# Two weight splits moved behind four bank sums, and the last norm's variance computed with tokens on partitions

## The reference

```python
attn = softmax((x @ Wq) @ (x @ Wk).T * scale) @ (x @ Wv) @ Wp + bp
cms  = gelu(attn @ cW1 + cb1) @ cW2 + cb2 + one_hot(codes)      # hidden size 2048
mod  = gelu(concat(attn, cms) @ mW1 + mb1) @ mW2 + mb2
x    = clip(x + cms + mod, 0, 1)

h    = x + gelu(x @ Wd[role] + bd) @ Wu[role] + bu              # adapter, 256 wide
mean = h.mean(-1); var = ((h - mean) ** 2).mean(-1)
x    = (h - mean) * rsqrt(var + 1e-5) * gamma[role] + beta[role]
```

## Time and profile before

| | |
|---|---|
| median of three runs | 2097.38 us (2095.5 to 2100.05) |
| the profiled execution | 2097.53 us |
| its span, first to last instruction | 2095.8 us |
| mean granted TensorE clock | 0.998 |
| TensorE matmul busy | 2073.3 us (99%), 9128 records |
| VectorE busy | 1588.5 us (76%) |
| ScalarE busy | 1097.1 us (52%) |
| GpSimd busy | 701.6 us (33%) |

### The profile page before, as it was taken

The page is one execution under the profiler, slowest core; times in us unless marked ns, Lnnn a source line. Parts: engine busy times, 40 slices in busy tenths (PEclk is TensorE's granted clock), DMA queues, the critical chain, the costliest instruction groups (busy, mean ns, idle before and its releaser), DMA issues.

```text
span 2095.8 us, 25018 instructions
## 1 busy us (share of the span) xinstructions
PE 2073.3 (99%) x9128; PEld 1701.9 (81%) x9128; DVE 1588.5 (76%) x1929; ACT 1097.1 (52%) x1625; POOL 701.6 (33%) x690
## 2 busy tenths in 40 slices
PE   9999999999999999999999999999999999999997
PEld 7887888888888888888888888888888888888884
DVE  4358878777868878867787887977686888787776
ACT  5366645454447654544454755544444666454444
POOL 1254415674002331766100332455400042165510
PEclk9999999999999999999999999999999999999999
DMA  8895444543212425444403222322130423421111
GB/s 304 239 236 143 133 114 120 130 119 101 103 46 105 154 76 138 114 113 103 129 30 133 88 71 83 99 61 61 45 127 0 151 74 104 115 61 59 52 61 41
DMA packets 183993, 221.94 MB, mean 106 GB/s; under 512 B 10288, under 2 KB 148272, under 8 KB 179776
## 3 DMA queue, kind: packets, MB, share of 16 engines
q1 hardware_dynamic: 175776, 184.58, 27.1%
q0 software_dynamic: 6720, 29.47, 7.8%
q10 hardware_dynamic: 1376, 6.29, 0.8%
HBM read 199.33 MB, written 62.91 MB: 125 GB/s over the span
## 4 chain that ended last, share of the span: by engine, by line
PE 93%; DVE 4%; ACT 1%; DMA 1%; issue 1%; SPq 0%; ACTq 0%; DVEq 0%
PE bank L864 30%; PE bank L866 30%; PE bank L865 30%; PE bank L919 1%; DMA stage<-ready_up 1%; DVE ring L1757 1%; DVE pc L2032 1%; PE bank L1262 1%; DVE xs L2207 0%; ACT ring L1298 0%; DMA fold_staging<-fold_w 0%; DVE ph_lo L2015 0%; PE bank L1233 0%; PE bank L1232 0%; PE bank L1231 0%
## 5 line engine op out<-in xcount | busy, mean ns | idle before, releaser
L1757 DVE TENSOR_TENSOR ring<-stage,ring 128x1024 fp32r<-128x1024 f32 (+1 forms) x288 | 356.1, 1246 | 67.2 <-ACT ring L1298 67.0
L864 PE MATMUL bank<-xa,ring 128*128 128x512 f32 x1016 | 396.1, 390 | 1.8 <-DVE raw_odd L1943 1.4
L866 PE MATMUL bank<-xa,ring 128*128 128x512 f32 x1016 | 395.3, 389 | 0.0
L865 PE MATMUL bank<-xa,ring 128*128 128x512 f32 x1016 | 395.3, 389 | 0.0
L864 PE MATMUL bank<-ph_hi,ring 128*128 128x512 f32 x808 | 317.1, 392 | 3.8 <-DVE pc L2032 1.8
L1298 ACT ACTIVATE ring<-stage 128x1024 fp32r<-128x1024 f32 (+1 forms) x288 | 271.8, 964 | 86.3 <-PE bank L866 40.2
L865 PE MATMUL bank<-ph_lo,ring 128*128 128x512 f32 x808 | 314.5, 389 | 0.0
L866 PE MATMUL bank<-ph_hi,ring 128*128 128x512 f32 x808 | 314.5, 389 | 0.0
L864 PE MATMUL bank<-vc,ring 128*128 128x512 f32 x672 | 261.7, 390 | 0.2
L866 PE MATMUL bank<-vc,ring 128*128 128x512 f32 x672 | 261.5, 389 | 0.0
L865 PE MATMUL bank<-vc,ring 128*128 128x512 f32 x672 | 261.4, 389 | 0.0
(11 more groups left out here) (202 smaller groups left out, 3698.6 us busy)
## 6 DMA issues: line engine op xcount, KB each, us to landing
stage<-ready_up SPq DMA_DIRECT2D x40, 896.0 KB, 5.2
stage<-mod_w SPq DMA_DIRECT2D x112, 256.0 KB, 3.4
stage_pair<-ready_pair SPq DMA_DIRECT2D x12, 1792.0 KB, 9.8
stage<-mod_w SPq DMA_DIRECT2D x28, 512.0 KB, 4.9
ready_up<-ready_up POOLq DMA_DIRECT2D x100, 128.0 KB, 5.1
ready_up<-cms_w SPq DMA_DIRECT2D x98, 128.0 KB, 3.4
ready_pair<-cms_w SPq DMA_DIRECT2D x42, 256.0 KB, 5.8
stage<-folded SPq DMA_DIRECT2D x16, 512.0 KB, 5.6
```

What stands on the lines that cost most here:

```text
L864: pe.matmul(dst, lh, rh, start=start and n == 0, stop=False, skip_group_check=not start)
L865: pe.matmul(dst, lh, rl, start=False, stop=False, skip_group_check=not start)
L866: done = pe.matmul(dst, ll, rh, start=False, stop=n == last, skip_group_check=not start)
L1757: dve.tensor_tensor(ring_part(key, 1), staged(key), f32(ring_part(key, 0)), ALU.subtract).then_inc(w_lo, 1)
```

## The change

Two edits. First, on VectorE, the two splits at the end of `cms_last` go behind the four bank sums at the head of `cms_end`, in all four rounds. Second, in the last norm alone, the variance is taken with the squares as the stationary operand and one column of `mean_f` as the moving one: for every k and every block j of 128 tokens, one matmul of 128x128 by 128x1 into column j of the bank, 16 for each b in place of four of 128x512. The variance then is a 128x4 tile with tokens on partitions. Square root and reciprocal run on 128x4. To bring it back over the features, VectorE makes a diagonal matrix of 128x128 for each of the four token blocks (identity times 1/std times 512, into `raw`), and one plain fp32 matmul of `mean_f` by the 128x512 diagonals (`last_wide`) writes 1/std of every token into all partitions of the bank. The scaling reads that bank instead of `lsum`. `last_wide(0)`, `last_variance(1)` and `last_wide(1)` stand at the end of TensorE's program; on VectorE `last_factors(0)` (reciprocal and diagonals) stands ahead of centre 1, and `last_factors(1)` behind scale 0.

```diff
 cms_last (VectorE)
                 hidden_lo(r, n, 2)
-                split_lo((r, "A", n + 1, 1))
-                split_lo((r, "C", n + 1, 1))
 cms_end (VectorE)
                 for m in range(KT):
                     down_add(r, n, 0, m)
+                split_lo((r, "A", n + 1, 1))
+                split_lo((r, "C", n + 1, 1))
                 operand_lo(vc, B11, pc[:, 0, 0:2, :], cms_hi, t0 + 1, cms_lo)
...
 TensorE
+            def last_variance(b):
+                for k in range(KT):
+                    pe.wait_ge(squared, (ROUNDS - 1) * GROUP * KT + KT * b + k + 1)
+                    for j in range(T // P):
+                        done = pe.matmul(bank[6 + b][:, j:j + 1], pc[:, b, k, j * P:(j + 1) * P], mean_f[:, 0:1],
+                                         start=k == 0 and j == 0, stop=k == KT - 1, skip_group_check=True)
+                done.then_inc(stat_done, 1)
+            def last_wide(b):
+                pe.wait_ge(diag_ready, T // P * (b + 1))
+                pe.matmul(bank[6 + b][:, :], mean_f[:, :], diag(b), start=True, stop=True).then_inc(wide_ready, 1)
             def last_amid(m):
...
                 if m == 2:
-                    last_stat(1, 0)
+                    last_variance(0)
...
-            last_stat(1, 1)
+            last_wide(0)
+            last_variance(1)
+            last_wide(1)
 ScalarE
-                norm_std(ROUNDS - 1, (6, 7), (2, 4), (b,))
+                act.wait_ge(stat_done, (ROUNDS - 1) * 4 + (2, 4)[b])
+                act.activation(lsum[:, b, 0:T // P], bank[6 + b][:, 0:T // P], ACT.Sqrt, bias=eps[:, :]).then_inc(std_ready, 1)
 VectorE
+            def last_factors(b):
+                dve.wait_ge(std_ready, r * GROUP + b + 1)
+                dve.reciprocal(lsum[:, b, 0:T // P], lsum[:, b, 0:T // P]).then_inc(rstd_ready, 1)
+                dve.wait_ge(rstd_ready, r * GROUP + b + 1)
+                for j in range(T // P):
+                    dve.tensor_scalar(diag(b)[:, j * P:(j + 1) * P], ident[:, :], lsum[:, b, j:j + 1], float(D),
+                                      ALU.mult, ALU.mult).then_inc(diag_ready, 1)
+            def last_scale(b):
+                dve.wait_ge(wide_ready, b + 1)
+                for k in range(KT):
+                    dve.tensor_tensor(xs[:, b, k, :], xs[:, b, k, :], bank[6 + b][:, :], ALU.mult).then_inc(scaled, 1)
             r = ROUNDS - 1
+            last_factors(0)
             norm_centre(r, 1, 3)
-            for b in range(GROUP):
-                norm_rstd(r, b)
-                norm_scale(r, b)
+            last_scale(0)
+            last_factors(1)
+            last_scale(1)
```

More of the change, by code:

```diff
@@ L396, in build @@
                              "std_ready", "rstd_ready", "scaled", "x_final"))
+        diag_ready, wide_ready = sem("diag_ready"), sem("wide_ready")
         out_done = sem("out_done")
@@ L425, in block_lo, with diag @@
             return t[:, LO_AT[block] + j:LO_AT[block] + j + n, :]
+        def diag(b):
+            return raw[:, b, :]
         FOLD_ORDER = (0, 2, 1, 3)
@@ L1252, in adapt, with last_mean @@
                             between(m)
-            def last_stat(what, b, tiles=range(KT)):
-                r = ROUNDS - 1
+            def last_mean(b, tiles=range(KT)):
                 for k in tiles:
[L1257 to L1263, removed]
+                    pe.wait_ge(ada_added, (ROUNDS - 1) * GROUP * KT + KT * b + k + 1)
+                    done = pe.matmul(bank[4 + b][:, :], mean_f[:, :], xs[:, b, k, :], start=k == 0, stop=k == KT - 1)
                     if k == KT - 1:
                         done.then_inc(stat_done, 1)
+            def last_variance(b):
[8 more added lines that the diff above has]
+                pe.matmul(bank[6 + b][:, :], mean_f[:, :], diag(b), start=True, stop=True).then_inc(wide_ready, 1)
             def last_amid(m):
                 if m == 0:
-                    last_stat(0, 0)
+                    last_mean(0)
                 else:
-                    last_stat(0, 1, range(m - 1, m) if m < KT - 1 else range(m - 1, KT))
+                    last_mean(1, range(m - 1, m) if m < KT - 1 else range(m - 1, KT))
                 if m == 2:
-                    last_stat(1, 0)
+                    last_variance(0)
             pe.wait_ge(mean_set, 1)
@@ L1674, in norm_squares, with norm_std @@
                     act.activation(raw[:, n % 2, :], xs[:, n // KT, n % KT, :], ACT.Square).then_inc(squared, 1)
-            def norm_std(r, banks, at=(3, 4), batches=range(GROUP)):
-                for b in batches:
-                    act.wait_ge(stat_done, r * 4 + at[b])
+            def norm_std(r, banks):
+                for b in range(GROUP):
+                    act.wait_ge(stat_done, r * 4 + 3 + b)
                     act.activation(lsum[:, b, :], bank[banks[b]][:, :], ACT.Sqrt, bias=eps[:, :]).then_inc(std_ready, 1)
```

## The result

The changed kernel took 2103.77 us (median of ten runs, 2101.42 to 2106.76), the kernel before 2098.11 us beside it on the same chip: a ratio of 1.003 [1.0022, 1.0038], 0.3% **slower**, 5.7 us by the medians. The forecast was 2091.7 us. The profiled execution of the changed kernel took 2106.76 us (span 2105.1, mean granted clock 0.994); that is the slowest of its ten, 3 us over the median, so single rows say where the time went and the medians how much. Six of the ten executions show a mean granted clock of 0.996 or 0.997 and took 2101.42 to 2104.09 us; the other four show 0.994 or 0.995 and took 2105.25 to 2106.76 us. The profiled one is of these four.

A forecast was written before the change was run, and what follows sets the result against it. The prediction took TensorE, 93% of the chain, as the bound, then its waits for bank sums and VectorE's chain at the end. -1.65 - 0.1 - 4.1 = -5.85 us gave 2091.7 us, range 2089.3 to 2097.3.

The forecast's parts named there:

- Part 1, the gap: TensorE's wait for the bank sums, 0.41 us lost in each of four rounds, goes when sums precede splits.
- Part 1, the cover: SyncE's weight loads, held some 3 us longer by two stage buffers, still come in time; some 8 us of slack.
- The term of -1.65 us: Gain from moving the bank sums ahead of the splits: four rounds by 0.41 us, bounds 0 to -2.5.
- part 1 gives nothing: Rival: a later wait in the same slot takes the 0.41 us, or delayed loads come late; 2093.4 us, chance 0.07.
- Its sign: What would show the forecast wrong here: a wait of TensorE in slot 8 on line 1757 or 1799.
- Part 2, the small terms: Last norm: square root 0.3 us, reciprocal 0.19, factors 0.94 in all, one-column matmul 0.21, scale 2.5.
- the prediction's formula: The skill's fp32 VectorE formula, (N + 151)/0.96 ns: a diagonal 0.29 us, the factors 1.35 us instead of 0.94.
- Part 2, the clock: Rival in the last norm: TensorE's clock falls under one-column matmuls, making it slower; chance 0.22, a third in full.
- The prediction's row of slow weight loads: Loads at the program's start take 0.33 us against 0.19, read as loads slowing down at the slow clock.
- the forecast's -4.2: In the last norm, scale 1 starts at 2085.5 instead of 2089.73; the program's end moves by -4.1 us.
- the full price of +7.3 us: Clock falls in variance 0 and stays down: m = 3, mean, variance 1 and wide matmul all pay; 2099.0 us.
- The smaller form, +4.2: Only variance 1 (3.3 us) and the wide matmul (0.9) pay for the fallen clock, called likelier; 2095.9 us.

The follow-up runs named there:

- e3: Kernel before with only the first of the four bank sums ahead of the two splits, old norm: 2095.42 us, ratio 0.9995.
- e4: e1 with GpSimd's residual adds cut to 64 columns each, so most of the residual is left out: 2095.73 us in one run.
- e8: Kernel before with three bank sums ahead of the two splits and the fourth behind them, old norm: 2096.36 us, ratio 0.9995.
- e1: Kernel before with all four bank sums ahead of the two splits, old norm: 2103.46 us, ratio 1.0033.
- e2: Kernel before with the new last norm alone, sums and splits in their old order: 2095.97 us, ratio 0.9997.
- e5: Changed kernel with only the first bank sum ahead of the splits, new norm kept: 2094.83 us, ratio 0.9989 to the kernel before.
- e7: e2 with the squares and the column in fp32r, two columns wide, 16 weight loads per variance instead of 32: 2093.39 us, ratio 0.9978.
- e6: e2 with variance 0 cut in two halves, real matmuls between them: 2094.73 us, ratio 0.9987 to the kernel before.
- e9: e5 with the edits of e6 and e7 added (variance 0 in halves, squares in fp32r): 2090.48 us, ratio 0.9969 to the kernel before.

## Why the prediction was wrong, step by step

**Part 1, the gap: right.** The wait for the sums went, the next matmul came 0.23 us behind, and e3 keeps a gain of 0.5 us a round in its profile, 2.1 us in all where -1.65 was forecast. The 0.1 us a round beyond the gap itself was not traced.

**Part 1, the cover: this step failed.** "SyncE is held some 3 us longer by the two buffers" was exact (3.0 us). "That cover is wide" was not, and neither was "the loads have some 8 us of slack, so this is weak". I took the slack from loads that land in 7 us, and that is the middle one of three. The third, which ScalarE waits for, took 19.4 to 19.7 us in the kernel before, beside GpSimd's residual, and landed only 2.9 to 3.1 us before ScalarE took it; with the gap closed ScalarE wants it 0.5 us sooner, so some 2.5 us were left. The change took 2.95 us by the later issue and 0.9 to 1.8 us by a longer landing. Of the residual adds the text says that they wait for `added` "which comes earlier", as if that were harmless: it puts 2 MB of GpSimd's DMA on the engines 1.2 us sooner, beside loads that come 3 us later. No run parts what the sooner residual adds to the landing from what the later loads add. e4 shows that the load is late only because the residual's transfers are beside it, e3 and e8 that the loss grows with the delay of the issue once the slack is gone. The term of -1.65 us was in truth +6.2 by the rounds (6.9 by e1's median): 2.1 won at the gaps, 8.2 lost as ScalarE gets its weights 1.6, 2.2, 2.1 and 2.3 us late. The copies behind the loads in SyncE's queue, which I named as the cover, have no part in it: rounds 2 and 3 have none at this place and lose as much.

The Trainium skill ("DMA: Bandwidth & Descriptors", the section that issuing engines are not separate DMA queues) says that transfers started by different engines run on the same 16 DMA engines and interleave there. It is the rule that spoke against this step, and I had not weighed it; the traces here agree, with 21.3 us for the third load beside the residual against 9.9 without it (e4), and that section gives no price for it.

The rival "part 1 gives nothing" named the place (the delayed loads come late), but it was priced at zero at worst and given 7%. Nothing in the list of rivals let it end at +6. Its sign did come, in slots 8 and 9: waits of TensorE on the split's line.

**Part 2, the small terms: right.** Square root of 128x4 0.26 us (0.3 forecast), reciprocal 0.17 to 0.18, four diagonals 0.88 from the first start, so the factors take about 1.1 us with their gap instead of 0.94 (in e2 a diagonal starts 0.20 us after the one before, not 0.17; it is booked with 0.28 to 0.29 us, as the prediction's formula gave, but its estimate of 1.35 lacked the overlap); scale 1 from the bank 2.48. One column is 0.22 us at full clock (two records that start 0.11 us apart in e2), as taken from the transposes (0.21). The Trainium skill ("TensorE: Matmul & The Clock Gate", its section on LDWEIGHTS) gives a load as its number of columns over 1.2, in ns, which makes 107 ns for 128 columns by our arithmetic. The distance between starts agrees; the single load is booked with 0.19 us.

**Part 2, the clock: the rival came true in part.** "TensorE is never idle in variance 0" was the argument against it. The rows show that this did not protect it: under records of one column the engine is booked busy for 2.00 of 2.00 us, and the granted clock falls to 0.50 all the same. (The prediction's row of slow weight loads, 0.33 us at the program's start, is no evidence of a low clock, as the windows there show 1.00; but the changed kernel's loads do take 0.33 us at 0.50.) In e2 the price was 1.5 us ahead of the mean's end and 1.1 in the wide matmul (2.08 instead of 1.02); after, it was 3.2 and more. From the mean's end to the program's end the forecast was 13.5 us; e2 has 14.84 and the changed kernel 16.8, against 17.6 before. The median of e2 keeps -0.6 us of the forecast's -4.2. Against the forecast's stretch of 28.3 us from the first mean to the end, e2's profile is 2.9 us over, e5's 6.2 and the changed kernel's 6.5, so the full price of +7.3 us came near in two profiles of three. The smaller form, +4.2, is close to the 3.6 us that e2's median lacks, but by luck: it put all of it on variance 1 and the wide matmul, and in e2 variance 1 ran at full clock (3.73 us) while m = 3 and the mean paid.

**The sum.** With the measured terms, +6.9 (e1's median) and -0.6 (e2's) give +6.3 us. The changed kernel's median lies 5.7 us over that of the kernel before beside it. The runs ask for no further term, though the intervals (2 us and more either way) leave room for one.

**What stays open.** Why the clock falls some 3 us into variance 0 in one execution (the changed kernel's) and only behind it in another of the same instructions (e2's); no run here controls it. Nor was it tried to hold the residual adds back instead of the loads, or to load the third piece first, which would show whether its place behind the other two costs it the time.

## What to carry to other kernels

A step that is moved takes its buffers' releases with it. For each transfer that these start, find the one that a later engine waits for, and read its slack as the time from its own landing to the instruction that takes it; the median of a group hid a load of 19.7 us behind one of 7.3 here. Then ask what else will be on the DMA engines, whatever queue it comes from. When a stall is one wait for one instruction, move that one instruction only: one sum of four closed the gap here, and each further sum only used up the slack of the third load. And a busy TensorE is not a TensorE at full clock: where matmuls of a few columns follow one another, have fewer of them in a row or full ones between, and price what stands behind them at either clock.

## What the runs showed of the hardware

Three loads of 896 KB are issued within 1.1 us, and GpSimd's accumulating DMAs, 2 MB in all, start on another queue up to 4 us behind the first. The middle load lands after 7.2 to 7.7 us from 3.4 us of lead on (before, e3), 10.9 to 14.4 at 2.1 to 2.2 (e8), 18.7 to 19.6 at none (after). The third takes 19.4 to 21.3 us in all of these, and 9.7 to 11.1 with the residual cut (e4). The engines are near full either way, but move fewer bytes while both kinds run. Windows of the changed kernel in round 1, the columns as above:

```profile
812.00:816.00 4.00, 4.00 (x20) 3.30 (x19) 4.00 (x5) 2.63 (x3) 0.98 (x2) 1.00 1.04 223
...
824.00:828.00 4.00, 4.00 (x20) 3.30 (x19) 1.72 (x2) 0.00 (x0) 0.00 (x0) 1.00 1.09 370
```

A full DMA share means some 220 GB/s while the residual is beside the loads and 370 behind it; the kernel before shows 221 from 810 to 814 us as well. That the accumulating is what slows it was not tried by itself.

And sixteen weight loads with their narrow matmuls (variance 0 of e7, 2.24 us, with full matmuls behind it) left the clock at 1.00, thirty-two in a row (3.6 us and more) did not in any of the three profiles that have them for variance 0 (after, e2, e5), and two times sixteen with full matmuls between (e6) did. It is no guarantee: in e9 variance 1, also sixteen, met a falling clock (2.75 us instead of about 2.2).
